# Attention scores on 64-row halves of TensorE's array, placed behind each step's transposes

## The chip, the cores and the metric

The kernel runs on one core of one Trainium2 chip. The time is device microseconds (us) of that core; lower is better. Before the change the median of three runs is 4348.14 us.

## What is computed

Two layers, each a group normalisation, an eight-head self-attention over 1024 positions and an output projection with a residual. The batch is 8, the channels 512, so a head has D = 64. All data are float32. One layer, cut to what matters (the second has another weight layout and the same mathematics):

```python
xn = group_norm(xf, norm_w, norm_b)                       # xf: (8, 512, 1024), 32 groups
qkv = einsum('oc,bct->bot', qkv_w, xn) + qkv_b            # 8 heads of q, k, v, 64 rows each
weight = softmax(einsum('bct,bcs->bts', q, k) / sqrt(64), axis=-1)
a = einsum('bts,bcs->bct', weight, v)
x = xf + einsum('oc,bct->bot', proj_w, a) + proj_b
```

## The kernel before

**Precision.** A float32 product is made from two fp32r parts, a high part (a rounded copy) and a low part (the rest), as three matmuls: high by high, high by low, low by high. So every tensor that TensorE multiplies has a `_hi` and a `_lo` form.

**Passes, pairs, steps, tiles.** A pass is one image in one layer: 2 x 8 = 16 passes (`Fori(0, PASSES)`). A pass has 8 heads in 4 pairs. Three pairs are run by an inner loop (`last` false), the fourth is written out (`last` true). So there are 48 loop pairs and 16 last pairs. A pair has 16 steps m (head e = 0 or 1, j = 0 to 7 in it), and a step is one tile of 128 queries against 1024 keys: 1024 tiles in all. Heads of Q and K for the head after next are projected in the loop pairs (`later_qk`, 3 matmuls a step, 6 in step 15); in the last pair a part of the output projection stands there in steps 0, 1, 14 and 15. A pass begins with the projections of V and of the first heads, and ends with the output projection.

**One tile's way.** TensorE writes the scores of tile m into half m % 2 of `ps_s`. DVE takes the row extreme (`smallest`, L560, `row_min`). ACT takes the exponential into `probs`, with the row sum by an accumulator read (`exponential`, L479). DVE takes the reciprocal (`reciprocal`, L564, `row_rcp`). POOL multiplies (`normalise`, L383). TensorE transposes the 1024 columns in 8 blocks into the two banks of `ps_t` (`transpose`, L760). ACT copies each bank as fp32r (`high_part`, L484, `pt_hi`, half 0 and half 1), DVE subtracts (`low_part`, L569, `pt_lo`, half 0 and half 1). After two tiles TensorE multiplies V with them into `ps_o` (`weigh`, L772 and L773, 8 matmuls a step from step 2 on; group 7 with 16 matmuls behind step 15). V stands with its high part in columns 0 to 63 and its low part in 64 to 127 (`v_st`), so `ps_o` holds two 64-row halves that must be added: ACT copies one (`other_half`, L491, `o_part`), DVE adds (`add_halves`, L578, `attn`), and then ACT and POOL split `attn` (`attn_high` L500, `attn_split` L407). For 4 of the 8 groups the sum goes to rows 0 to 63, for the others to rows 64 to 127.

**Scores before.** Q's high and low part are stacked to 128 rows (`q_st`), K's high part stands twice (`kh_st`) and K's low part stands twice (`kl_st`). Four matmuls of 128 x 512 make a tile's scores (L749 and L751, two column halves). POOL splits Q and K (`split_qk`, L370 and L372), and SP stacks them with two DMAs, a wait on them (`q_moved`), and two more (`stack`, L259 to L267); they write into the places that they read.

**Order.** It is written out by hand, the same in every engine. Each engine runs its own instructions strictly as listed and waits on semaphores. TensorE in step m: scores of tile m + 2, transposes of m, later Q and K, weigh. DVE in step m: (in even steps from 4 on, in a loop pair) `add_halves`; `smallest(m+2)`, `low_part(m, 0)`, `low_part(m, 1)`, `reciprocal(m+2)`. `scores` of m + 2 waits for the exponential of m; a transpose half waits for `low_part` of the tile before; `exponential(m+2)` waits for `smallest(m+2)`. ACT's order, which the change leaves as it is, is:

```python
                        if not last and m >= 4 and m % 2 == 0:
                            other_half(8 * pair + m // 2 - 2, m // 2 - 2)
                        high_part(tile + m, m, 0)
                        high_part(tile + m, m, 1)
                        if m == PT_STEPS - 1 or last and m >= 3 and m % 2 == 1:
                            other_half(8 * pair + (m - 3) // 2, (m - 3) // 2)
                        if not (last and m + 2 >= PT_STEPS):
                            exponential(tile + m + 2, m + 2, 2 * (tile + m) + 2)
                        if j in (3, 7) and not last:
                            evac_qk(hd + 2, col + hh + 2, j // 4, g_bank, True)
                        if j == 2 and not (last and e == 1):
                            v_high(hd + 1, hh + 1, 1 - e, 4 * hd)
                        if e == 1 and j in (4, 6):
                            attn_high(pair, p, (j - 4) // 2)
```

`evac_qk` (L466) takes the next Q and K out of PSUM, `v_high` (L473) copies V. Behind step 15 of a pair ACT has `attn_high(2)`, `other_half(7)` and `attn_high(3)`, DVE `add_halves(7)`. POOL in step m has at most one or two splits (`split_qk`, `split_wqk` L347 and L349, `v_low` L377, `attn_split`) and then `normalise(m+2)`. V's bias is added when V leaves PSUM (`evac_v`, L631, from `bv_all`).

Of the kernel before, what the change touches and what calls it, by code (L numbers as in the profile page):

```python
# [7 lines left out]
F32 = mybir.dt.float32  # L28
# [36 lines left out]
def build(nc, x, wqk, wv, wp, bqk, bv, bo, nw, nb, consts, out):  # L65
    mid = nc.dram_tensor("layer0_out", (B, C, T), F32, kind="Internal").ap()

    with ExitStack() as ctx:
# [34 lines left out]
        q_st = [sb(f"q_st{s}", [P, T], F32R) for s in range(2)]  # L103
        kh_st = [sb(f"kh_st{s}", [P, T], F32R) for s in range(2)]
        kl_st = [sb(f"kl_st{s}", [P, T], F32R) for s in range(2)]
# [8 lines left out]
        bv_all = sb("bv_all", [P, LAYERS, C], F32)  # L114
# [4 lines left out]
        bo_sb = sb("bo_sb", [P, LAYERS * KT], F32)  # L119
        nw_sb = sb("nw_sb", [P, LAYERS * KT], F32)  # L120
        nb_sb = sb("nb_sb", [P, LAYERS * KT], F32)
        qk_scale = sb("qk_scale", [P, 1], F32)
        row_min = sb("row_min", [P, 4], F32)
        row_sum = sb("row_sum", [P, 4], F32)
        row_rcp = sb("row_rcp", [P, 4], F32)
# [38 lines left out]
        q_moved = sem("q_moved")  # L164
# [81 lines left out]
        def _(sp):  # L246
# [34 lines left out]
            sp.dma_start(bv_all[:, :, :], bv.rearrange("(o l) n -> o l n", o=1).broadcast_to([P, LAYERS, C])).then_inc(const_loaded, 16)  # L281
# [61 lines left out]
        def _(pool):  # L343
# [22 lines left out]
            def split_qk(hd, s, half):  # L366
# [3 lines left out]
                nc.gpsimd.tensor_scalar(kh_st[s][:, cols], qk[:, cols], 1.0, 1.0, ALU.mult, ALU.mult).then_inc(qk_hi_done, 1)  # L370
                pool.wait_ge(qk_hi_done, 2 * hd + half + 1)
                nc.gpsimd.tensor_tensor(kl_st[s][:, cols], qk[:, cols], f32(kh_st[s][:, cols]),  # L372
# [183 lines left out]
        def _(dve):  # L556
# [15 lines left out]
            def add_halves(pair, k):  # L572
# [56 lines left out]
            def evac_v(i, lay, b):  # L629
# [34 lines left out]
            def pair_steps(i, p, last):  # L664
                pair = PAIRS * i + p
                tile = TILES * i + PT_STEPS * p
                for m in range(PT_STEPS):
                    if not last and m >= 4 and m % 2 == 0:
                        add_halves(pair, m // 2 - 2)
                    if not (last and m + 2 >= PT_STEPS):  # L670
                        smallest(tile + m + 2, m + 2)
                    low_part(tile + m, m, 0)
# [13 lines left out]
                add_halves(pair, 7)  # L686

            with dve.Fori(0, PASSES) as i:
                lay = i // B
                for b in range(4):  # L690
                    evac_v(i, lay, b)
                for m in range(2):
                    smallest(TILES * i + m, m)
                    evac_v(i, lay, 4 + 2 * m)
                    reciprocal(TILES * i + m, m)
                    evac_v(i, lay, 5 + 2 * m)
                with dve.Fori(0, PAIRS - 1) as p:
                    pair_steps(i, p, False)
# [237 lines left out]
```

## Time and profile before

| | |
|---|---|
| median of 3 runs | 4348.14 us (4347.87 to 4348.57) |
| span of the profiled execution, first to last instruction | 4346.0 us |
| matmuls (PE) | 26692, PE busy 99% |
| DVE, ACT, POOL busy | 76%, 66%, 58% |
| mean granted TensorE clock | 0.999 of full speed |

For the profiled execution the span is what is listed; the median of the runs lies 2.1 us above it. PE is TensorE's matmuls, PEld its weight loads, DVE VectorE, ACT ScalarE, POOL GpSimd, SP the engine that issues the DMAs. Busy shares are means over stages with different limits, so the rows below go to single stages. A matmul's duration overlaps the next one's, so the distance from start to start is what a matmul costs.

### The profile page before, as it was taken

Reading aid. Unit: us, or ns where it says so; the run is one execution under the profiler, and the core shown is the slowest. Engines: PE = TensorE matmul, PEld = TensorE weight load, DVE = VectorE, ACT = ScalarE, POOL = GpSimd, SP = SyncE. Lnnn points to the kernel's source line nnn. Section 1 sums busy time; section 2 is a strip of 40 time slices with the busy share of each in tenths; the row PEclk is TensorE's granted clock in tenths of the full one; section 3 lists DMA queues with packets and bytes.
Section 4 is the critical chain, followed back from the end, with each engine's and each line's share of the span. In section 5 each row is a group of like instructions: output and inputs, shape, how many; then the busy total and the mean of one; then the engine's idle time right before and its main releaser. Section 6 shows DMA issues by size and latency. Waiting matters only on the chain.

```text
span 4346.0 us, 89905 instructions
## 1 busy us (share of the span) xinstructions
PE 4295.6 (99%) x26692; PEld 3736.9 (86%) x26692; DVE 3313.6 (76%) x5483; ACT 2875.3 (66%) x5317; POOL 2505.1 (58%) x2406
## 2 busy tenths in 40 slices
PE   7999999999999999999999999999999999999999
PEld 6888888888888888888888888888888888888887
DVE  5777867788687786777867778687786877868778
ACT  4757747477474775747757476574765747667476
POOL 5655556565564655656566565565655646556465
PEclk9999999999999999999999999999999999999999
DMA  3232222322223222222222222222222222223222
GB/s 87 48 96 47 71 72 48 96 47 80 64 46 96 49 78 64 56 86 49 80 71 66 81 46 80 65 66 79 48 79 64 71 71 49 79 64 82 60 49 92
DMA packets 99933, 295.61 MB, mean 68 GB/s; under 512 B 15136, under 2 KB 15264, under 8 KB 99616
## 3 DMA queue, kind: packets, MB, share of 16 engines
q1 hardware_dynamic: 99616, 291.71, 25.0%
q8 instruction: 158, 2.59, 0.3%
q14 instruction: 159, 1.30, 0.1%
HBM read 123.88 MB, written 33.55 MB: 36 GB/s over the span
## 4 chain that ended last, share of the span: by engine, by line
PE 95%; DVE 2%; issue 1%; POOL 1%; ACT 1%; DMA 0%; SPq 0%; DVEq 0%; ACTq 0%; POOLq 0%
PE ps_t L760 21%; PE ps_g L714 15%; PE ps_o L772 11%; PE ps_o L773 11%; PE ps_s L751 11%; PE ps_s L749 11%; PE ps_s L714 7%; PE ps_t L714 6%; PE ps_o L714 3%; POOL x_raw L389 1%; ACT probs L479 0%; DVE spread L603 0%; DVE pt_lo L569 0%; DVE work L601 0%; PE ps_t L778 0%
## 5 line engine op out<-in xcount | busy, mean ns | idle before, releaser
L383 POOL TENSOR_SCALAR probs<-probs,row_rcp 128x1024 f32<-128x1024 f32 x1024 | 1149.9, 1123 | 1375.5 <-DVE row_rcp L564 1374.0
L560 DVE TENSOR_REDUCE row_min<-ps_s 128x1 f32<-128x1024 f32 x1024 | 1250.2, 1221 | 220.5 <-PE ps_s L751 205.0
L484 ACT CAST pt_hi<-ps_t 128x512 fp32r<-128x512 f32 x2048 | 1110.6, 590 | 446.5 <-PE ps_t L760 431.7
L569 DVE TENSOR_TENSOR pt_lo<-ps_t,pt_hi 128x512 fp32r<-128x512 f32 x2048 | 1308.5, 679 | 9.5 <-ACT pt_hi L484 5.0
L479 ACT ACTIVATE probs<-ps_s,row_min 128x1024 f32<-128x1024 f32 x1024 | 1150.7, 1124 | 215.5 <-DVE row_min L560 202.5
L760 PEld LDWEIGHTS ps_t<-const_sb,probs 128*128 128x128 f32 x8192 | 944.3, 140 | 185.5 <-DVE pt_lo L569 57.0
L760 PE MATMUL ps_t<-const_sb,probs 128*128 128x128 f32 x8192 | 1085.9, 274 | 0.8
L772 PE MATMUL ps_o<-pt_hi,v_st 128*128 128x256 f32 x4096 | 1044.4, 288 | 0.0
L773 PE MATMUL ps_o<-pt_lo,v_st 128*128 128x256 f32 x4096 | 1014.8, 282 | 0.0
L751 PE MATMUL ps_s<-kl_st,q_st 128*128 128x512 f32 x2048 | 808.3, 395 | 0.0
L772 PEld LDWEIGHTS ps_o<-pt_hi,v_st 128*128 128x128 f32 x4096 | 771.6, 188 | 39.4 <-issue 12.4
L749 PE MATMUL ps_s<-kh_st,q_st 128*128 128x512 f32 x2048 | 804.1, 393 | 0.0
L773 PEld LDWEIGHTS ps_o<-pt_lo,v_st 128*128 128x128 f32 x4096 | 774.4, 189 | 29.0
L751 PEld LDWEIGHTS ps_s<-kl_st,q_st 128*128 128x128 f32 x2048 | 388.0, 189 | 54.9
L578 DVE TENSOR_TENSOR attn<-ps_o,o_part 64x256 f32<-64x256 f32 x512 | 215.5, 421 | 281.3 <-ACT o_part L491 276.3
L749 PEld LDWEIGHTS ps_s<-kh_st,q_st 128*128 128x128 f32 x2048 | 386.0, 188 | 50.1 <-DMA kl_st<-kl_st 0.2
L714 PE MATMUL ps_g<-xn_hi,wqk_hi 128*128 128x512 f32 x768 | 352.8, 459 | 0.0
L372 POOL TENSOR_TENSOR kl_st<-qk,kh_st 128x512 fp32r<-128x512 f32 x256 | 329.6, 1287 | 21.4
L491 ACT COPY o_part<-ps_o 64x256 f32<-64x256 f32 x512 | 187.6, 366 | 186.2 <-PE ps_o L773 179.2
L564 DVE RECIPROCAL row_rcp<-row_sum 128x1 f32<-128x1 f32 x1024 | 167.5, 164 | 183.8 <-ACT probs L479 150.2
L714 PE MATMUL ps_g<-xn_hi,wqk_lo 128*128 128x512 f32 x768 | 307.2, 400 | 0.0
L714 PE MATMUL ps_g<-xn_lo,wqk_hi 128*128 128x512 f32 x768 | 304.3, 396 | 0.0
(110 smaller groups left out, 4918.2 us busy)
## 6 DMA issues: line engine op xcount, KB each, us to landing
wqk_raw<-in_wqk SPq DMA_DIRECT2D x130, 256.0 KB, 2.7
q_st<-kh_st SPq DMA_DIRECT2D x128, 256.0 KB, 2.9
q_st<-kl_st SPq DMA_DIRECT2D x128, 256.0 KB, 3.6
kh_st<-kh_st SPq DMA_DIRECT2D x128, 256.0 KB, 2.9
kl_st<-kl_st SPq DMA_DIRECT2D x128, 256.0 KB, 3.5
x_raw<-layer_out SPq DMA_DIRECT2D x36, 512.0 KB, 5.0
wv_raw<-in_wv SPq DMA_DIRECT2D x68, 256.0 KB, 3.6
x_raw<-in_x SPq DMA_DIRECT2D x32, 512.0 KB, 5.3
```

Source lines behind the costliest of these rows:

```text
L372: nc.gpsimd.tensor_tensor(kl_st[s][:, cols], qk[:, cols], f32(kh_st[s][:, cols]), ALU.subtract).then_inc(qk_split, 1)
L383: nc.gpsimd.tensor_scalar(probs[m % 2][:, :], probs[m % 2][:, :], row_rcp[:, m % 4:m % 4 + 1], 1.0, ALU.mult, ALU.mult).then_inc(probs_rea ...
L479: nc.scalar.activation(probs[m % 2][:, :], ps_s[:, m % 2, :], ACT.Exp, bias=row_min[:, m % 4:m % 4 + 1], scale=-1.0, accum_out=row_sum[:, ...
L484: nc.scalar.copy(pt_hi[:, m // 2 % 2, 4 * half:4 * half + 4, (m % 2) * P:(m % 2 + 1) * P], ps_t[:, half, :].rearrange("p (b t) -> p b t", ...
L560: nc.vector.tensor_reduce(row_min[:, m % 4:m % 4 + 1], ps_s[:, m % 2, :], AX.X, ALU.min).then_inc(min_ready, 1)
L569: nc.vector.tensor_tensor(pt_lo[place], ps_t[:, half, :].rearrange("p (b t) -> p b t", b=4), f32(pt_hi[place]), ALU.subtract).then_inc(lo_ ...
L714: return nc.tensor.matmul(bank, stat[hi_lo[0]](n // 3), mov[hi_lo[1]](n // 3), start=first, stop=last)
L749: nc.tensor.matmul(ps_s[:, m % 2, cols], q_st[s][:, j * P:(j + 1) * P], kh_st[s][:, cols], start=True, stop=False)
L751: mm = nc.tensor.matmul(ps_s[:, m % 2, cols], q_st[s][:, j * P:(j + 1) * P], kl_st[s][:, cols], start=False, stop=True)
L760: mm = nc.tensor.transpose(ps_t[:, half, b * P:(b + 1) * P], probs[m % 2][:, (4 * half + b) * P:(4 * half + b + 1) * P], ident)
L772: nc.tensor.matmul(ps_o[:, 0:GROUP], v, pt_hi[:, k % 2, b, :], start=(b == 0), stop=False)
L773: mm = nc.tensor.matmul(ps_o[:, 0:GROUP], v, pt_lo[:, k % 2, b, :], start=False, stop=(b == BLK - 1))
```

## The change

Scores: Q's and K's high parts stay as POOL writes them (`hi_st`: Q in rows 0 to 63, K in rows 64 to 127), the low parts too (`lo_st`), and four DMAs put swapped copies beside them (`hi_sw`, `lo_sw`), with no wait between. A tile's scores are six matmuls of 64 rows by 512 columns, in three pairs: one of a pair uses rows 0 to 63 of the array and makes columns 0 to 511, the other uses rows 64 to 127 and makes columns 512 to 1023. A pair is one of the three products.

Order: TensorE has `transpose(m)` ahead of `scores(m+2)`. DVE has `low_part(m, 0)`, `reciprocal(m+1)`, `smallest(m+2)`, `low_part(m, 1)`; the reciprocal of tile 1 of a pass moves from the head of the pass into step 0. ACT's and POOL's orders stay.

V's bias: no longer added to V, but to the sum of the halves (the probabilities of a row add up to 1), so `evac_v` becomes a copy and `add_halves` an operation with three inputs. The small tiles `qk_scale`, `row_min`, `row_sum`, `row_rcp` become slices of one, `row_stats`.

```diff
@@ SP, stack
-                sp.dma_start(f32(q_st[s][0:D, :]), f32(kh_st[s][0:D, :])).then_inc(q_moved, 16)
-                sp.dma_start(f32(q_st[s][D:P, :]), f32(kl_st[s][0:D, :])).then_inc(q_moved, 16)
-                sp.wait_ge(q_moved, 32 * (hd + 1))
-                sp.dma_start(f32(kh_st[s][0:D, :]), f32(kh_st[s][D:P, :])).then_inc(stacked[s], 16)
-                sp.dma_start(f32(kl_st[s][0:D, :]), f32(kl_st[s][D:P, :])).then_inc(stacked[s], 16)
+                for swapped, straight in ((hi_sw, hi_st), (lo_sw, lo_st)):
+                    sp.dma_start(f32(swapped[s][D:P, :]), f32(straight[s][0:D, :])).then_inc(stacked[s], 16)
+                    sp.dma_start(f32(swapped[s][0:D, 0:HALF]), f32(straight[s][D:P, 0:HALF])).then_inc(stacked[s], 16)
...
-            sp.dma_start(bv_all[:, :, :], bv.rearrange("(o l) n -> o l n", o=1).broadcast_to([P, LAYERS, C])).then_inc(const_loaded, 16)
+            sp.dma_start(bv_sb[:, :], bv).then_inc(const_loaded, 16)
@@ DVE, add_halves and evac_v
-                nc.vector.tensor_tensor(attn[rows, cols], ps_o[rows, 0:GROUP], o_part[k % 2][rows, :],
-                                        ALU.add).then_inc(attn_ready, 1)
+                nc.vector.scalar_tensor_tensor(out=attn[rows, cols], in0=ps_o[rows, 0:GROUP],
+                                               scalar=bv_sb[rows, bass.ds(lay * KT + p, 1)], in1=o_part[k % 2][rows, :],
+                                               op0=ALU.add, op1=ALU.add).then_inc(attn_ready, 1)
...
-                nc.vector.tensor_tensor(v_raw[:, b, :].rearrange("p (o n) -> p o n", o=1),
-                                        v_bank[b].rearrange("p (o n) -> p o n", o=1),
-                                        bv_all[:, bass.ds(lay, 1), :], ALU.add).then_inc(v_evac, 1)
+                nc.vector.tensor_copy(v_raw[:, b, :], v_bank[b]).then_inc(v_evac, 1)
@@ DVE, pair_steps
-                    if not (last and m + 2 >= PT_STEPS):
-                        smallest(tile + m + 2, m + 2)
                     low_part(tile + m, m, 0)
+                    if not (last and m + 1 >= PT_STEPS):
+                        reciprocal(tile + m + 1, m + 1)
+                    if not (last and m + 2 >= PT_STEPS):
+                        smallest(tile + m + 2, m + 2)
                     low_part(tile + m, m, 1)
                     if m == PT_STEPS - 1 or last and m >= 3 and m % 2 == 1:
-                        add_halves(pair, (m - 3) // 2)
-                    if not (last and m + 2 >= PT_STEPS):
-                        reciprocal(tile + m + 2, m + 2)
+                        add_halves(pair, lay, p, (m - 3) // 2)
@@ TensorE, scores
-                j = m % NT
-                for half in range(2):
-                    cols = slice(half * HALF, (half + 1) * HALF)
-                    nc.tensor.matmul(ps_s[:, m % 2, cols], q_st[s][:, j * P:(j + 1) * P], kh_st[s][:, cols],
-                                     start=True, stop=False)
-                    mm = nc.tensor.matmul(ps_s[:, m % 2, cols], q_st[s][:, j * P:(j + 1) * P], kl_st[s][:, cols],
-                                          start=False, stop=True)
+                tile = slice((m % NT) * P, (m % NT + 1) * P)
+                top, low = slice(0, D), slice(D, P)
+                first, second = slice(0, HALF), slice(HALF, T)
+                for n, (q, k) in enumerate(((0, 0), (1, 0), (0, 1))):
+                    nc.tensor.matmul(ps_s[:, m % 2, first], (hi_st, lo_st)[q][s][top, tile],
+                                     (hi_sw, lo_sw)[k][s][top, first], start=n == 0, stop=n == 2)
+                    mm = nc.tensor.matmul(ps_s[:, m % 2, second], (hi_sw, lo_sw)[q][s][low, tile],
+                                          (hi_st, lo_st)[k][s][low, second], start=n == 0, stop=n == 2)
                 mm.then_inc(scores_ready, 1)
@@ TensorE, pair_steps
+                        transpose(tile + m, m)
                         if not (last and m + 2 >= PT_STEPS):
                             pe.wait_ge(exp_ready, tile + m + 1)
...
                             scores(m + 2, s)
...
-                        transpose(tile + m, m)
```

How the change moves DVE's instructions shows in a step of a loop pair that has no `add_halves`. In these rows `ISA` and `REGISTER_ALU` are waits on semaphores and their counters, the rest are as named above. DVE before, from the `smallest` of one step to that of the next:

```order
L560 TENSOR_REDUCE row_min<-ps_s 128x1
L567 ISA
L569 TENSOR_TENSOR pt_lo<-ps_t,pt_hi 128x4x128
L567 REGISTER_ALU
L569 TENSOR_TENSOR pt_lo<-ps_t,pt_hi 128x4x128
L564 RECIPROCAL row_rcp<-row_sum 128x1
L559 REGISTER_ALU
L560 TENSOR_REDUCE row_min<-ps_s 128x1
```

DVE with the change, from the `low_part(m, 0)` of one step to the `smallest` of the next:

```order
L546 TENSOR_TENSOR pt_lo<-ps_t,pt_hi 128x4x128
L540 REGISTER_ALU
L541 RECIPROCAL row_stats<-row_stats 128x1
L536 REGISTER_ALU
L537 TENSOR_REDUCE row_stats<-ps_s 128x1
L544 REGISTER_ALU
L546 TENSOR_TENSOR pt_lo<-ps_t,pt_hi 128x4x128
L544 ISA
L546 TENSOR_TENSOR pt_lo<-ps_t,pt_hi 128x4x128
L541 RECIPROCAL row_stats<-row_stats 128x1
L536 REGISTER_ALU
L537 TENSOR_REDUCE row_stats<-ps_s 128x1
```

Before, the `smallest` stood ahead of both `low_part`s of its step; now one `low_part` and the reciprocal stand ahead of it and one `low_part` behind it.

TensorE before, from the end of one step's `weigh` to the `later_qk` of the next (`const_sb` is the identity that the transposes multiply with, and `x4` is four blocks):

```order
L773 MATMUL ps_o<-pt_lo,v_st_73 128x256
L811 REGISTER_ALU
L749 MATMUL ps_s<-kh_st_68,q_st_66 128x512
L751 MATMUL ps_s<-kl_st_70,q_st_66 128x512
L749 MATMUL ps_s<-kh_st_68,q_st_66 128x512
L751 MATMUL ps_s<-kl_st_70,q_st_66 128x512
L758 ISA
L760 MATMUL ps_t<-const_sb,probs_80 128x128 x4
L758 REGISTER_ALU
L760 MATMUL ps_t<-const_sb,probs_80 128x128 x4
```

TensorE with the change, the same stretch:

```order
L753 MATMUL ps_o<-pt_lo,v_st_75 128x256
L736 REGISTER_ALU
L738 ISA
L740 MATMUL ps_t<-const_sb,probs_83 128x128 x4
L738 REGISTER_ALU
L740 MATMUL ps_t<-const_sb,probs_83 128x128 x4
L729 MATMUL ps_s<-hi_sw_70,hi_st_66 128x512
L731 MATMUL ps_s<-hi_st_66,hi_sw_70 128x512
L729 MATMUL ps_s<-hi_sw_70,lo_st_68 128x512
L731 MATMUL ps_s<-hi_st_66,lo_sw_72 128x512
L729 MATMUL ps_s<-lo_sw_72,hi_st_66 128x512
L731 MATMUL ps_s<-lo_st_68,hi_sw_70 128x512
```

The scores moved behind the eight transposes, and four matmuls became six; L729 uses the array's upper rows and L731 its lower rows.

## Rows read from the trace of the kernel before

**Rows 1.** The page: span, PE busy, chain that ended last.

```profile
span 4346.0 us, 89905 instructions
...
PE 4295.6 (99%) x26692; PEld 3736.9 (86%) x26692; DVE 3313.6 (76%) x5483; ACT 2875.3 (66%) x5317; POOL 2505.1 (58%) x2406
...
PE 95%; DVE 2%; issue 1%; POOL 1%; ACT 1%; DMA 0%; SPq 0%; DVEq 0%; ACTq 0%; POOLq 0%
```

**Rows 2.** Windows table, loop pair and 14 last-pair steps: length, busy us (count), clock.

```profile
982.76:1038.05 55.29, 55.29 (x369) 49.32 (x368) 44.27 (x73) 43.57 (x82) 34.50 (x34) 1.00 0.22 53
1038.05:1078.68 40.63, 40.58 (x277) 34.81 (x275) 37.06 (x61) 34.33 (x65) 21.05 (x20) 1.00 0.35 110
```

**Rows 3.** Chain of waits, one step of a loop pair: start us, us, what.

```profile
1000.19 0.23 PE ps_s L749
...
1001.12 0.87 PE ps_t L760 x8
1002.00 0.69 PE ps_g L714 x3
1002.69 0.12 PE ps_o L772
...
1003.64 0.23 PE ps_s L749
```

**Rows 4.** Timeline of ACT, last pair: start us, us, operation [idle <-releaser].

```profile
1048.25 1.11 ACT L479 ACTIVATE probs<-ps_s,row_min 128x1024 f32<-128x1024 f32 x1
...
1049.36 1.06 ACT L484 CAST pt_hi<-ps_t 128x512 fp32r<-128x512 f32 x2
1050.84 1.12 ACT L479 ACTIVATE probs<-ps_s,row_min 128x1024 f32<-128x1024 f32 x1 [0.42 <-DVE row_min L560]
```

**Rows 5.** Timeline of DVE, a loop pair: low parts, reciprocal, smallest.

```profile
968.44 1.29 DVE L569 TENSOR_TENSOR pt_lo<-ps_t,pt_hi 128x512 fp32r<-128x512 f32 x2
969.68 0.16 DVE L564 RECIPROCAL row_rcp<-row_sum 128x1 f32<-128x1 f32 x1
969.78 1.23 DVE L560 TENSOR_REDUCE row_min<-ps_s 128x1 f32<-128x1024 f32 x1
```

**Rows 6.** Timeline of DVE, last pair: the smallest ahead of the exponential at 1050.84.

```profile
1049.59 1.22 DVE L560 TENSOR_REDUCE row_min<-ps_s 128x1 f32<-128x1024 f32 x1
```

**Rows 7.** Timeline of all engines, step 15: copy, waiting low part.

```profile
1081.13 1.07 ACT L484 CAST pt_hi<-ps_t 128x512 fp32r<-128x512 f32 x2 [1.08 <-PE ps_t L760]
...
1081.74 0.69 DVE L569 TENSOR_TENSOR pt_lo<-ps_t,pt_hi 128x512 fp32r<-128x512 f32 x1
```

**Rows 8.** Timeline of ACT: what else stands between exponential and copy.

```profile
981.31 0.36 ACT L491 COPY o_part<-ps_o 64x256 f32<-64x256 f32 x1 [0.84 <-PE ps_o L773]
...
982.76 1.07 ACT L484 CAST pt_hi<-ps_t 128x512 fp32r<-128x512 f32 x2
...
1007.10 0.79 ACT L466 ACTIVATE qk<-ps_g,bqk_sc,qk_scale 128x512 f32<-128x512 f32 x1
1007.92 0.37 ACT L491 COPY o_part<-ps_o 64x256 f32<-64x256 f32 x1
...
1045.91 0.61 ACT L473 CAST v_st<-v_raw 128x512 fp32r<-128x512 f32 x1
1046.47 1.07 ACT L484 CAST pt_hi<-ps_t 128x512 fp32r<-128x512 f32 x2
...
1075.43 0.39 ACT L500 CAST a_hi<-attn 128x256 fp32r<-128x256 f32 x1
1075.72 1.09 ACT L484 CAST pt_hi<-ps_t 128x512 fp32r<-128x512 f32 x2
```

**Rows 9.** The page: normalise on POOL, a score matmul, a stacking DMA.

```profile
L383 POOL TENSOR_SCALAR probs<-probs,row_rcp 128x1024 f32<-128x1024 f32 x1024 | 1149.9, 1123 | 1375.5 <-DVE row_rcp L564 1374.0
...
L751 PE MATMUL ps_s<-kl_st,q_st 128*128 128x512 f32 x2048 | 808.3, 395 | 0.0
...
kl_st<-kl_st SPq DMA_DIRECT2D x128, 256.0 KB, 3.5
```

More of the change, by code:

```diff
@@ L102, in build @@
         qk = sb("qk", [P, T], F32)
-        q_st = [sb(f"q_st{s}", [P, T], F32R) for s in range(2)]
-        kh_st = [sb(f"kh_st{s}", [P, T], F32R) for s in range(2)]
-        kl_st = [sb(f"kl_st{s}", [P, T], F32R) for s in range(2)]
+        hi_st = [sb(f"hi_st{s}", [P, T], F32R) for s in range(2)]
+        lo_st = [sb(f"lo_st{s}", [P, T], F32R) for s in range(2)]
+        hi_sw = [sb(f"hi_sw{s}", [P, T], F32R) for s in range(2)]
+        lo_sw = [sb(f"lo_sw{s}", [P, T], F32R) for s in range(2)]
         v_raw = sb("v_raw", [P, BLK, C], F32)
@@ L119, in build @@
         bo_sb = sb("bo_sb", [P, LAYERS * KT], F32)
+        bv_sb = sb("bv_sb", [P, LAYERS * KT], F32)
         nw_sb = sb("nw_sb", [P, LAYERS * KT], F32)
         nb_sb = sb("nb_sb", [P, LAYERS * KT], F32)
[L122 to L125, printed above, removed]
+        row_stats = sb("row_stats", [P, 16], F32)
+        qk_scale = row_stats[:, 12:13]
+        row_min, row_sum, row_rcp = (row_stats[:, 4 * n:4 * n + 4] for n in range(3))
         bn_part = sb("bn_part", [P, KT, 12], F32)
@@ L570, in low_part, with add_halves @@
                                         f32(pt_hi[place]), ALU.subtract).then_inc(lo_ready, 1)
-            def add_halves(pair, k):
+            def add_halves(pair, lay, p, k):
                 rows = slice(0, D) if k < 4 else slice(D, P)
@@ L662, in _, with pair_steps @@
                 x_low(0, c)
-            def pair_steps(i, p, last):
+            def pair_steps(i, lay, p, last):
                 pair = PAIRS * i + p
@@ L668, in pair_steps @@
                     if not last and m >= 4 and m % 2 == 0:
-                        add_halves(pair, m // 2 - 2)
+                        add_halves(pair, lay, p, m // 2 - 2)
+                    low_part(tile + m, m, 0)
+                    if not (last and m + 1 >= PT_STEPS):
+                        reciprocal(tile + m + 1, m + 1)
                     if not (last and m + 2 >= PT_STEPS):
                         smallest(tile + m + 2, m + 2)
-                    low_part(tile + m, m, 0)
                     low_part(tile + m, m, 1)
                     if m == PT_STEPS - 1 or last and m >= 3 and m % 2 == 1:
-                        add_halves(pair, (m - 3) // 2)
-                    if not (last and m + 2 >= PT_STEPS):
-                        reciprocal(tile + m + 2, m + 2)
+                        add_halves(pair, lay, p, (m - 3) // 2)
                     if last and m == PT_STEPS - 2:
@@ L685, in pair_steps @@
                     group_spread(i + 1)
-                add_halves(pair, 7)
+                add_halves(pair, lay, p, 7)
             with dve.Fori(0, PASSES) as i:
@@ L690, in _ @@
                 for b in range(4):
-                    evac_v(i, lay, b)
+                    evac_v(i, b)
                 for m in range(2):
                     smallest(TILES * i + m, m)
-                    evac_v(i, lay, 4 + 2 * m)
-                    reciprocal(TILES * i + m, m)
-                    evac_v(i, lay, 5 + 2 * m)
+                    evac_v(i, 4 + 2 * m)
+                    if m == 0:
+                        reciprocal(TILES * i, 0)
+                    evac_v(i, 5 + 2 * m)
                 with dve.Fori(0, PAIRS - 1) as p:
-                    pair_steps(i, p, False)
-                pair_steps(i, PAIRS - 1, True)
+                    pair_steps(i, lay, p, False)
+                pair_steps(i, lay, PAIRS - 1, True)
                 norm_coefs(i + 1, within(next_pass(i) // B, 0, LAYERS - 1))
@@ L858, in _ @@
                     qk_part(half, qk_bank[1][half], 1, 0, 3 * KT)
-                pe.wait_ge(stacked[0], 32 * (4 * i + 1))
+                pe.wait_ge(stacked[0], 64 * (4 * i + 1))
                 scores(0, 0)
```

12 lines of the change are left out of this document (5 added, 7 removed).

## The prediction, made before the changed kernel ran

> **What bounds the kernel now.** First the page: TensorE is busy 99% of the span and 95% of the chain that ended last [rows 1]. Such a share is a mean, so next the windows: TensorE is busy all of a loop pair's 55.29 us and nearly all of the 40.63 us of steps 0 to 13 of a last pair, at full clock (the column behind the busy times) [rows 2]. The chain of waits then gives one loop step by starts: scores 0.93 us (1000.19 to 1001.12), eight transposes 0.88, three matmuls for later Q and K 0.69, weigh 0.95, together 3.45 us [rows 3]. So in a loop pair each microsecond saved on TensorE is one saved, if nothing else is longer.
>
> In the last pair something else is nearly as long. There ACT sat idle for 0.42 us before the exponential at 1050.84, waiting for DVE's smallest [rows 4]. Here one must ask not how busy DVE and ACT are, but which of their instructions wait for each other in turn. Today the turn is: exponential, reciprocal, smallest of the next tile, exponential. It leaves out the copy and the low part, since DVE's list has the smallest ahead of them.
>
> **What the change does to TensorE.** A score matmul costs 0.23 us from start to start [rows 3]. Four become three pairs. If the halves run side by side, a tile's scores cost 3 x 0.23 = 0.69 instead of 0.93: 0.24 us less per tile, 1024 x 0.23 = about 236 us in all. If they run one after the other, six cost 1.38, 0.45 more. No row shows a 64-row matmul, so these two are my bounds; I take the first, but below it hardly counts. A change between full and half array may cost nothing or, by the nearest row, the tail by which a score matmul outlasts its start-to-start distance: 0.395 - 0.23 = 0.16 us [rows 3, 9], twice a step.
>
> **What it does to DVE and ACT.** This is the term that decides. DVE now has low_part(m, 0), reciprocal(m+1), smallest(m+2), low_part(m, 1). ACT still has copy(m, 0), copy(m, 1), exponential(m+2). Follow one turn: exponential(m+2) on ACT is ahead of copy(m+1, 0) on ACT; that is awaited by low_part(m+1, 0) on DVE; behind that in DVE's list are reciprocal(m+2) and smallest(m+3); and that is awaited by exponential(m+3). This is a ring of one step in which nothing can overlap, whatever TensorE does. Its length from rows:
> - exponential to next copy, start to start: 1.11 (1048.25 to 1049.36) [rows 4]
> - copy to a low part that waits for it: 0.61 (1081.13 to 1081.74) [rows 7]
> - low part to reciprocal: two low parts last 1.29 and one 0.69, so the second starts 0.60 behind the first, and the reciprocal 1.24 - 0.60 = 0.64 behind the second [rows 5, 7]
> - reciprocal to smallest: 0.10 [rows 5]
> - smallest to exponential: 1.25 (1049.59 to 1050.84) [rows 4, 6]
>
> Sum 3.71 us, against TensorE's new step of 0.69 + 0.88 + 0.69 + 0.95 = 3.21. The ring wins, and TensorE begins to wait.
>
> Whatever ACT does between an exponential and the next copy lengthens the ring. In a loop pair [rows 8]: four evacuations of Q and K at 0.8 (0.82 to the next start), 3.2; six other_half ahead of a copy at 0.4 (0.37 and its handover), 2.4; two copies of V at 0.56, 1.1; two of attn at 0.29, 0.6. add_halves on DVE runs beside the copy (0.61) and is hidden. At the pair's end: from copy(15, 0), the exponential of tile 17 starts at +2.60, the evacuation ends at +4.5, attn_high(2) at +4.8, and TensorE finishes group 7 at about +5.0 (an estimate: 0.88 + 0.69 + 0.95 + 6 x 0.23 + 16 x 0.12 = 5.8 of its work, begun some 0.8 ahead of the copy). Then other_half(7), add_halves(7), attn_high(3) to the next pair's copy take 1.45 as now (981.31 to 982.76). That is +6.45, where an ordinary step would be at +4.5: 1.95 more. One loop pair: 16 x 3.71 + 3.2 + 2.4 + 1.1 + 0.6 + 1.95 = 68.6 us, against 55.3: **+13.3, times 48 = +638**.
>
> Last pair, copy(0, 0) to copy(14, 0): 14 x 3.71 = 51.9, with one copy of V and one of attn 52.8, against 40.6 [rows 2]. The other_half there stands behind both copies, in ACT's time of waiting for the smallest, and is hidden. **+12.2, times 16 = +195**.
>
> **Edits that cost nothing.** evac_v and the first two tiles' scores lie at a pass's head, where DVE waits for TensorE: only the two score tiles count, -0.46 us a pass, -7. Should the copy be slower than the add, TensorE's next work there covers it. add_halves with a third input may be longer by a tenth (it has no row); the copy beside it has 0.2 to spare. The four stacking DMAs follow each other without the wait that stood between; one lands in 3.5 us [rows 9], and they have five steps. POOL's normalise waited 1374 us in all for the reciprocal [rows 9]: it will wait again, as its list is as before. The reciprocal now stands 0.10 ahead of the smallest, so normalise (1.12) is done while smallest and exponential run (2.36 to the copy), and the first transposes are just in time: some 0.4 us to spare. If that were used up, transposes would be late next. TensorE's spare time (about 0.5 a step) covers two array changes of 0.16.
>
> **Sum.** 4346 + 638 + 195 - 7 = 5172 us of span. The median of the runs stands 2 above the span of the profiled execution: 5174, and I say **5175**. Bounds of the ring: with every handover 0.02 shorter, 3.61; with the low part, the reciprocal and the smallest counted at full length 0.69 + 0.16 + 1.25 and 0.04 per handover, about 3.9. Over the 48 x 16 + 16 x 14 = 992 steps that is -100 and +190.
>
> **Rivals.**
> 1. *TensorE stays the bound, halves side by side.* The gain of 236 us then comes out: **4110 us, faster**. Place: each step's scores; price: 0.23; it decides once the ring is under 3.45. For it: the page, on which DVE and ACT have 24% and 34% free [rows 1]. Against it: free time in a ring can't be used. 4%.
> 2. *The ring holds and the halves do not run side by side* (the change doesn't do what it says). TensorE's step is 3.21 + 0.69 = 3.90, with two array changes of 0.16 4.22. In a loop pair about five of 16 steps carry nothing extra on ACT and are then set by TensorE: 240 steps x 0.2 to 0.5, +50 to +120 us, and more where the two chains couple: **about 5290**. For it: no row shows halves at all. 7%.
> 3. *TensorE stays the bound, and each array change costs its tail.* TensorE's step is 3.21 + 0.33, 0.09 longer than before: 4346 + 1024 x 0.09 = **about 4440, slower**. For it: the tail of 0.16 is in the rows. Against it: the ring is longer still. 3%.
>
> On this the Trainium skill has a rule, in "TensorEngine Tiling (Array Packing)", Key Properties under Tiling Modes: changing the tiling mode drains TensorE. By that rule rival 3 is how the change goes if only TensorE counts, and without the rule it is rival 1; the trace of before has only full-array matmuls and can't say. Beside the ring the rule changes nothing in the sum.
>
> **How the numbers follow.** The ring is a matter of the written order, and its parts are measured rows, so it gets 84% at 5175; 2% is left for what I don't see. The range takes in the ring's bounds and most of rival 2: 5060 to 5365. A measurement of this kernel can tell 0.2% (9 us) from no change. Faster 4% (rival 1), within 0.2% 1%, slower 95%.
>
> **What would show it.** Right: TensorE with idle time before the transposes or scores; ACT's copy waits little for TensorE; chains through exponential, copy, low part, smallest; the smallest-to-smallest distance in a last pair even, near 3.7 us; a loop pair near 68 us. Pairs of score matmuls starting close together and 0.23 us per pair show the halves side by side; 0.23 per matmul shows rival 2. Wrong: a loop pair under 56 us, or a chain that stays 90% TensorE, or copies that wait for transposes in most steps, which would put POOL's normalise in the ring's place.

## The result and the profile after

| | before | changed kernel |
|---|---|---|
| median | 4348.26 us (4347.87 to 4348.57, 4 runs) | 5235.68 us (5233.19 to 5238.03, 4 runs) |
| ratio | 1 | 1.2041, 95% interval 1.2024 to 1.2058 |
| span of the profiled execution | 4346.0 us | 5232.3 us |
| mean granted clock | 0.999 | 0.995 |

The change makes the kernel 887 us slower. The forecast was 5175, range 5060 to 5365.

The page of the changed kernel, against [rows 1, 9] (a group's columns: busy us, mean ns of one, idle us before them and their releaser):

```profile
span 5232.3 us, 94049 instructions
...
PE 4655.5 (89%) x28740; PEld 3547.1 (68%) x28740; DVE 3261.2 (62%) x5483; ACT 2854.5 (55%) x5317; POOL 2505.8 (48%) x2406
...
issue 28%; DVE 26%; PE 21%; ACT 17%; POOL 3%; ACTq 2%; DVEq 2%; DMA 0%; POOLq 0%; SPq 0%
...
L546 DVE TENSOR_TENSOR pt_lo<-ps_t,pt_hi 128x512 fp32r<-128x512 f32 x2048 | 1402.8, 686 | 927.6 <-ACT pt_hi L461 913.9
L456 ACT ACTIVATE probs<-ps_s,row_stats 128x1024 f32<-128x1024 f32 x1024 | 1143.4, 1117 | 1374.7 <-DVE row_stats L537 1366.7
L740 PE MATMUL ps_t<-const_sb,probs 128*128 128x128 f32 x8192 | 1114.0, 279 | 512.1 <-POOL probs L360 509.7
```

TensorE fell from 95% of the chain to 21%. DVE and ACT did not become busier: DVE is at 62% and ACT at 55%, less than before, yet together with "issue" (time in which an engine waited for nothing that the profile shows) they hold most of the chain. The three groups say who waits: the low part 914 us for the copy, the exponential 1367 us for the smallest, the transposes 510 us for the normalise. A ring in which each waits for the last looks like this. Before, the exponential waited 202.5 us in all for the smallest and the low part 5.0 for the copy.

Windows of the changed kernel, to be read against [rows 2]: two loop pairs, the stretch from a last pair's step 0 to the start of the next pass's second loop pair, and steps 0 to 13 of that last pair (length first, clock behind the counts):

```profile
1431.49:1500.42 68.93, 61.12 (x403) 46.09 (x400) 43.46 (x72) 43.45 (x82) 34.53 (x34) 1.00 0.12 31
1174.89:1245.01 70.12, 62.60 (x400) 47.22 (x400) 43.57 (x72) 43.58 (x83) 34.51 (x34) 0.98 0.13 38
1245.01:1431.49 186.48, 167.46 (x1000) 128.42 (x996) 114.80 (x196) 91.11 (x169) 85.48 (x80) 1.00 0.19 60
...
1245.01:1297.62 52.61, 43.23 (x298) 31.95 (x295) 37.24 (x62) 33.41 (x66) 22.79 (x22) 1.00 0.22 75
```

Between the starts of pairs, two loop pairs and the long stretch (last pair, output projection, head of the pass, first loop pair) make a pass. Over all that the trace shows, a loop pair went from 55.33 to 69.20 us (32 of each) and the long stretch from 158.67 to 186.40 (15 of each): 32 x 13.87 + 16 x 27.73 = 888, all of the loss. Of the 27.73, 13.87 is the loop pair in it and 11.98 are steps 0 to 13 of the last pair (40.63 to 52.61).

The ring, in a timeline of all engines of the changed kernel (start us, us, operation, [idle <-releaser]):

```profile
1132.66 1.12 ACT L456 ACTIVATE probs<-ps_s,row_stats 128x1024 f32<-128x1024 f32 x1 [1.46 <-DVE row_stats L537]
...
1132.96 1.09 PE L740 MATMUL ps_t<-const_sb,probs 128*128 128x128 f32 x8 [0.32 <-POOL probs L360]
...
1133.77 1.06 ACT L461 CAST pt_hi<-ps_t 128x512 fp32r<-128x512 f32 x2
...
1134.38 0.69 DVE L546 TENSOR_TENSOR pt_lo<-ps_t,pt_hi 128x512 fp32r<-128x512 f32 x1 [1.15 <-ACT pt_hi L461]
...
1134.98 0.15 DVE L541 RECIPROCAL row_stats<-row_stats 128x1 f32<-128x1 f32 x1
1135.06 1.20 DVE L537 TENSOR_REDUCE row_stats<-ps_s 128x1 f32<-128x1024 f32 x1
...
1136.29 1.11 ACT L456 ACTIVATE probs<-ps_s,row_stats 128x1024 f32<-128x1024 f32 x1 [1.46 <-DVE row_stats L537]
```

Read it as distances: exponential to copy 1.11, copy to low part 0.61, to reciprocal 0.60, to smallest 0.08, to the next exponential 1.23. That is 3.63 us for a step, and all of its links were named ahead. The copy at 1133.77 has no bracket: it waited for nothing but ACT's own exponential, although the transposes had begun only 0.81 ahead of it.

TensorE in the changed kernel, one step's transposes, scores and the first matmul for later Q and K:

```profile
1128.86 1.05 PE L740 MATMUL ps_t<-const_sb,probs 128*128 128x128 f32 x8
1129.84 0.49 PE L729 MATMUL ps_s<-hi_sw,hi_st 64*128 64x512 f32 x1
1129.84 0.49 PE L731 MATMUL ps_s<-hi_st,hi_sw 64*128 64x512 f32 x1
1130.17 0.39 PE L729 MATMUL ps_s<-hi_sw,lo_st 64*128 64x512 f32 x1
...
1130.73 0.50 PE L692 MATMUL ps_g<-xn_hi,wqk_hi 128*128 128x512 f32 x1
1131.07 0.40 PE L692 MATMUL ps_g<-xn_lo,wqk_hi 128*128 128x512 f32 x1
```

The halves do run side by side: both of a pair start within 0.01 us. But the first pair stands 0.33 ahead of the second (the next distance is 0.23), and the first full-array matmul behind them 0.34 ahead of the next, against 0.23 between such matmuls before. So TensorE's own step is 0.98 + 0.89 + 0.80 + 0.95 = 3.62 us here (transposes, scores, later Q and K, weigh), not 3.21, and not less than the 3.45 of before. Two things are thus to be separated: the ring and the halves.

### The profile page after: what moved, and what is told of

Same layout as the page of the kernel before. It is cut to its first block, busy times and chain, and to the rows that moved or that the text cites. A ratio compares the mean times of both kernels' runs of the same rounds, so it can differ in the third digit from the quotient of the medians.

```text
span 5232.3 us, 94049 instructions
## 1 busy us (share of the span) xinstructions
PE 4655.5 (89%) x28740; PEld 3547.1 (68%) x28740; DVE 3261.2 (62%) x5483; ACT 2854.5 (55%) x5317; POOL 2505.8 (48%) x2406
## 4 chain that ended last, share of the span: by engine, by line
issue 28%; DVE 26%; PE 21%; ACT 17%; POOL 3%; ACTq 2%; DVEq 2%; DMA 0%; POOLq 0%; SPq 0%
DVE row_stats L537 19%; ACT pt_hi L461 9%; PE ps_s L692 5%; ACT probs L456 5%; PE ps_t L692 4%; PE ps_o L752 2%; DVE row_stats L541 2%; PE ps_t L740 2%; ACT o_part L468 2%; PE ps_o L692 2%; PE ps_s L729 2%; POOL probs L360 2%; PE ps_g L692 2%; PE ps_o L753 2%; DVE pt_lo L546 1%
## 5 line engine op out<-in xcount | busy, mean ns | idle before, releaser
L360 POOL TENSOR_SCALAR probs<-probs,row_stats 128x1024 f32<-128x1024 f32 x1024 | 1151.3, 1124 | 2335.4 <-DVE row_stats L541 2335.4
L456 ACT ACTIVATE probs<-ps_s,row_stats 128x1024 f32<-128x1024 f32 x1024 | 1143.4, 1117 | 1374.7 <-DVE row_stats L537 1366.7
L537 DVE TENSOR_REDUCE row_stats<-ps_s 128x1 f32<-128x1024 f32 x1024 | 1234.9, 1206 | 101.5 <-PE ps_s L731 101.0
L729 PE MATMUL ps_s<-hi_sw,hi_st 64*128 64x512 f32 x1024 | 510.5, 499 | 0.0
L731 PE MATMUL ps_s<-hi_st,hi_sw 64*128 64x512 f32 x1024 | 509.8, 498 | 0.0
L729 PE MATMUL ps_s<-hi_sw,lo_st 64*128 64x512 f32 x1024 | 404.7, 395 | 0.0
L731 PE MATMUL ps_s<-hi_st,lo_sw 64*128 64x512 f32 x1024 | 404.3, 395 | 0.0
L729 PE MATMUL ps_s<-lo_sw,hi_st 64*128 64x512 f32 x1024 | 402.9, 393 | 0.0
L731 PE MATMUL ps_s<-lo_st,hi_sw 64*128 64x512 f32 x1024 | 402.6, 393 | 0.0
L349 POOL TENSOR_TENSOR lo_st<-qk,hi_st 128x512 fp32r<-128x512 f32 x256 | 328.9, 1285 | 21.4
```

The lines of the kernel that those rows point to most:

```text
L349: nc.gpsimd.tensor_tensor(lo_st[s][:, cols], qk[:, cols], f32(hi_st[s][:, cols]), ALU.subtract).then_inc(qk_split, 1)
L360: nc.gpsimd.tensor_scalar(probs[m % 2][:, :], probs[m % 2][:, :], row_rcp[:, m % 4:m % 4 + 1], 1.0, ALU.mult, ALU.mult).then_inc(probs_rea ...
L456: nc.scalar.activation(probs[m % 2][:, :], ps_s[:, m % 2, :], ACT.Exp, bias=row_min[:, m % 4:m % 4 + 1], scale=-1.0, accum_out=row_sum[:, ...
L537: nc.vector.tensor_reduce(row_min[:, m % 4:m % 4 + 1], ps_s[:, m % 2, :], AX.X, ALU.min).then_inc(min_ready, 1)
L729: nc.tensor.matmul(ps_s[:, m % 2, first], (hi_st, lo_st)[q][s][top, tile], (hi_sw, lo_sw)[k][s][top, first], start=n == 0, stop=n == 2)
L731: mm = nc.tensor.matmul(ps_s[:, m % 2, second], (hi_sw, lo_sw)[q][s][low, tile], (hi_st, lo_st)[k][s][low, second], start=n == 0, stop=n == 2)
```

## Experiments

Each is named by what it is made from. Single times are one execution, those with a range are several.

**1. Before, with DVE's new order alone.**

```diff
+                    low_part(tile + m, m, 0)
+                    if not (last and m + 1 >= PT_STEPS):
+                        reciprocal(tile + m + 1, m + 1)
                     if not (last and m + 2 >= PT_STEPS):
                         smallest(tile + m + 2, m + 2)
-                    low_part(tile + m, m, 0)
                     low_part(tile + m, m, 1)
                     if m == PT_STEPS - 1 or last and m >= 3 and m % 2 == 1:
                         add_halves(pair, (m - 3) // 2)
-                    if not (last and m + 2 >= PT_STEPS):
-                        reciprocal(tile + m + 2, m + 2)
...
-                    reciprocal(TILES * i + m, m)
+                    if m == 0:
+                        reciprocal(TILES * i, 0)
```

> The kernel before, with DVE's new order alone (low part 0, reciprocal of the next tile, smallest, low part 1); scores on the full array, TensorE's order as before. Theory of the ring (exponential, copy, low part, reciprocal, smallest, exponential, 3.63 us in the trace of the change): it is closed by DVE's order alone, so about 5200 us (5130 to 5260), smallest to smallest 3.63 us in plain steps. Rival, that the halves and the array changes around them cost the time: no halves here, so within 1% of 4348 us.

Measured: 5180.7 us. On its page TensorE is busy 89%, DVE 62% and ACT 55%, as in the change. Its waits (us in total, times, longest):

```profile
ACT probs L479 <- DVE row_min L560: 1484.8, 1024, 5.1
DVE pt_lo L569 <- ACT pt_hi L484: 925.8, 832, 1.7
```

Moving one low part and the reciprocal in DVE's list costs 832 of the 887 us, with TensorE's work untouched. A loop pair lasts 68.61 us, and a step in which ACT has nothing extra 3.63 to 3.64 from copy to copy.

**2. Before, with both new orders, full array** (experiment 1, and `transpose(m)` ahead of `scores(m+2)`).

> The change without the halves and without the moved bias: full-array scores, but the transposes ahead of the scores and DVE's new order. Ring: 5190 to 5240 us, as the change, since TensorE's step of 3.45 us is under the ring. Rival (halves are what costs): within 1% of 4348 us; a rival that the placement behind the transposes costs by itself shows as more than e1_new_dve_order_alone by over 50 us.

Measured: 5194.3 us. Putting the transposes first costs another 13 us. These are two single executions, but their traces agree: a loop pair is as long (68.66 us), and the long stretch goes from 184.16 to 184.88, 12 us over 16 passes. From here to the change, halves and bias add 41.

**3. The change, with both orders as before** (halves and moved bias stay).

> The change with TensorE's and DVE's orders as before: what halves and moved bias do by themselves. Ring: it is open again, TensorE binds, and a step costs what its work costs. In the trace of the change a step of TensorE's work is 3.62 us against 3.45 before, so about 4500 us (4440 to 4560), loop pairs near 58 us. If array changes cost less where the scores stand between weigh and transposes, down to 4110. Rival (halves are what costs): over 5000 us.

Measured: 4450.8 us (4449.5 to 4454.4, 4 runs), ratio 1.0233 (1.0216 to 1.0250). The chain of waits in a loop step, against [rows 3]:

```profile
2007.65 0.43 PE ps_s L728
...
2008.08 0.23 PE ps_s L728
...
2008.55 1.02 PE ps_t L739 x8
2009.57 0.70 PE ps_g L691 x3
...
2011.22 0.43 PE ps_s L728
```

TensorE holds 94% of this chain, so here its step decides: 3.57 us against 3.45. Three pairs would be 0.69; they take 0.89, since the first costs 0.43. The transposes behind them take 1.02 where they took 0.87. The two changes between full and half array cost 0.20 + 0.15 = 0.35, the halves give back 0.24.

**4. The bias alone** (before, with V's bias added in `add_halves`; the rest of the edit, the copy in `evac_v` among it, is cut here).

```diff
-                nc.vector.tensor_tensor(attn[rows, cols], ps_o[rows, 0:GROUP], o_part[k % 2][rows, :],
-                                        ALU.add).then_inc(attn_ready, 1)
+                nc.vector.scalar_tensor_tensor(out=attn[rows, cols], in0=ps_o[rows, 0:GROUP],
+                                               scalar=bv_sb[rows, bass.ds(lay * KT + p, 1)], in1=o_part[k % 2][rows, :],
+                                               op0=ALU.add, op1=ALU.add).then_inc(attn_ready, 1)
```

> The kernel before, with V's bias moved alone (copy out of PSUM, three-input add of the halves). Theory: hidden, 4348 us within 0.2%; the add of the halves takes 0.06 us longer as in the trace of the change (0.48 against 0.42), which no ring of before contains except at a pair's end (64 pairs x 0.06 = 4 us at most). Rival (the bias explains part of the 100 us that halves and bias together cost): 4370 us or more.

Measured: 4360.6 us (10 runs), ratio 1.0022 (1.0012 to 1.0031). That is 9 us over the 4351.5 of before in the same batch, and 12 over the 4348.8 of experiment 3's batch. It was to be hidden, 4 us at most, so this missed by a little. The add with three inputs takes 0.48 us against 0.42 in the groups by line, and a loop pair 55.56 against 55.33. So some 10 of experiment 3's 102 us are the bias, some 90 the halves.

**5. Experiment 3, with all six score matmuls on rows 0 to 63** (the DMAs then move the whole of K's swapped copy; that edit is not shown).

```diff
-                    mm = nc.tensor.matmul(ps_s[:, m % 2, second], (hi_sw, lo_sw)[q][s][low, tile],
-                                          (hi_st, lo_st)[k][s][low, second], start=n == 0, stop=n == 2)
+                    mm = nc.tensor.matmul(ps_s[:, m % 2, second], (hi_st, lo_st)[q][s][top, tile],
+                                          (hi_sw, lo_sw)[k][s][top, second], start=n == 0, stop=n == 2)
```

> Halves with both old orders, but all six matmuls of a tile on rows 0 to 63 (K's swapped copy is moved whole, so nothing is left out). If the two halves of the array really work side by side, taking that away costs 3 x 0.23 us a tile: 4451 + 1024 x 0.69 = 5157 us (5080 to 5180). Rival (the pairs' equal starts in the trace are only how matmuls are recorded, and they run one after the other): 4451 us unchanged.

Measured: 5147.6 us. TensorE's timeline in this kernel:

```profile
1100.98 0.50 PE L728 MATMUL ps_s<-hi_sw,hi_st 64*128 64x512 f32 x1
1101.32 0.39 PE L730 MATMUL ps_s<-hi_sw,hi_st 64*128 64x512 f32 x1
```

On the same rows the six follow one by one, the first 0.34 ahead of the second, the others 0.22 to 0.24 apart. That makes the kernel 697 us longer than experiment 3, near the 1024 x 0.69 = 707 of three matmuls more a tile. So it is the two row halves that let a pair share its 0.23.

**6 and 7. Four array changes a step instead of two, and the control.** Experiment 3 and the kernel before, each with its scores cut in two around the matmuls for later Q and K (one pair and two pairs; two matmuls and two). In experiment 3 (cut; the old place of `later_qk` is taken out and `scores` gets a range):

```diff
-                            scores(m + 2, s)
+                            scores(m + 2, s, 0, 1)
+                            if not last and m < PT_STEPS - 1:
+                                later_qk(i, m, hd, e, j)
+                            scores(m + 2, s, 1, 3)
```

> Halves with both old orders, and in loop pairs the three matmuls for later Q and K stand between the first pair of score matmuls and the other two: four array changes a step instead of two, the same matmuls. If two changes cost what the books say (0.24 gained, 0.12 lost in all, so 0.36 for two), 48 x 15 steps x 0.36 = 260 us more than e3_halves_both_orders_old, 4710 us (4640 to 4760), less what the same reordering costs with full-array scores (e8_full_split_around_qk). Rival (the loss comes from elsewhere, such as weight loads or DVE): no more than that control's difference.

> Control for e7_halves_split_around_qk: the kernel before, full-array scores, with the three matmuls for later Q and K between the two column halves of the scores. No array change at all, so what it costs is the reordering: 0 to 2 us a loop pair (the wait for the evacuation of Q and K comes 1.3 us earlier in four steps), 4348 to 4440 us.

Measured: 4917.8 us with halves, 4558.2 us for the control. The control missed: it was to cost at most 92 us and cost 210. Its waits (us in total, times, longest) say why:

```profile
PEld ps_g L714 <- ACT qk L466: 217.7, 144, 1.5
```

The matmuls for later Q and K now come before ACT has emptied their bank. With halves the same wait is 207.0 us, so it can be taken off. What is left for the array changes is the difference: halves cost 4917.8 - 4558.2 = 360 us with four changes a step and 4450.8 - 4348.8 = 102 with two. Those 258 us over the 720 steps of loop pairs in which the scores are cut (48 x 15) are 0.36 us for two more changes. In steps where nothing waits for the bank the traces give it without the control's loss: with halves a step goes from 3.57 to 3.97 us, in the control from 3.45 to 3.44, so 0.40 or 0.41 for two more changes. The change's own step (0.10 in the transposes, 0.20 in the scores, 0.11 in later Q and K over what they would take) gives 0.41. With the 0.35 of experiment 3's chain, two changes cost 0.35 to 0.41 us.

**8. The change, with DVE's order as before** (TensorE's transposes stay first).

> The change with DVE's order as before and TensorE's as changed (transposes ahead of scores). The ring between ACT and DVE is open, but the low part of a tile now stands behind the smallest of a tile whose scores come after the transposes: transposes 0.98, scores 0.89, arrival 0.2, smallest to low part 1.14, low part 0.69, together 3.9 us before the next transposes may start. So 4750 to 4950 us, loop pairs near 63 us, with transposes waiting for low parts. Rival (order does not matter): 5235 us as the change.

Measured: 5259.0 us. A clear miss: undoing what costs 832 us by itself gained nothing here. The timeline of all engines in this kernel:

```profile
1130.40 1.25 PE L739 MATMUL ps_t<-const_sb,probs 128*128 128x128 f32 x8 [0.30 <-DVE pt_lo L546]
...
1131.58 0.49 PE L728 MATMUL ps_s<-hi_sw,hi_st 64*128 64x512 f32 x1
...
1132.58 1.23 DVE L537 TENSOR_REDUCE row_stats<-ps_s 128x1 f32<-128x1024 f32 x1 [1.40 <-PE ps_s L730]
...
1133.73 1.28 DVE L546 TENSOR_TENSOR pt_lo<-ps_t,pt_hi 128x512 fp32r<-128x512 f32 x2
...
1134.46 1.25 PE L739 MATMUL ps_t<-const_sb,probs 128*128 128x128 f32 x8
```

This is another ring: transposes, scores (+1.18), smallest (+1.00), low part (+1.15), next transposes (+0.73), 4.06 us. The expectation had named it, with 3.9 us; the last pairs keep to it (56.08 us for 14 steps), but a loop pair takes 68.8 where 63 was expected, and why its steps with extra work on ACT and DVE take 4.4 to 5.05 was not traced. DVE has the smallest ahead of the low parts, TensorE the transposes ahead of the scores, so the transposes wait for a low part, that for the smallest, that for the scores, and those for the transposes. That a low part waits for the smallest holds only while DVE's smallest stands ahead of both low parts; with the new DVE order one low part stands ahead of it. So DVE's new order closes one ring, TensorE's new order with DVE's old one another, and the parts' costs don't add up. TensorE's new order alone on the full array was not run.

**9. The change, with a shorter smallest** (512 columns; it leaves out half of each row's search, so the exponential's shift comes from half a row).

```diff
-ps_s[:, m % 2, :], AX.X, ALU.min)
+ps_s[:, m % 2, 0:HALF], AX.X, ALU.min)
```

> The change, with the smallest taken over the first 512 of the 1024 columns (this leaves half of each row's search out; the exponential's shift then comes from half a row). One member of the ring is shortened by about 0.53 us (1.22 to 0.69, the length of DVE's other operations on 512 columns), nothing on TensorE. Theory of the ring: a plain step falls from 3.63 to 3.10 in the last pairs, where TensorE's work is below that; in loop pairs TensorE's own step of about 3.6 us takes over in plain steps and the ring stays where ACT has extra work, so 60 to 62 us a loop pair. In all about 4700 us (4640 to 4800). Rival (DVE is only 62% busy and so cannot bind): 5235 us within 1%.

Measured: 4965.9 us. Taking 0.53 us out of one link of the ring gained 270 us: the link is in the bound. But more was expected, and the timeline of this kernel shows what stopped it:

```profile
1201.74 0.15 DVE L541 RECIPROCAL row_stats<-row_stats 128x1 f32<-128x1 f32 x1
...
1202.10 1.12 POOL L360 TENSOR_SCALAR probs<-probs,row_stats 128x1024 f32<-128x1024 f32 x1 [2.83 <-DVE row_stats L541]
...
1203.35 1.09 PE L740 MATMUL ps_t<-const_sb,probs 128*128 128x128 f32 x8 [0.83 <-POOL probs L360]
...
1204.04 1.07 ACT L461 CAST pt_hi<-ps_t 128x512 fp32r<-128x512 f32 x2 [0.32 <-PE ps_t L740]
...
1205.27 0.15 DVE L541 RECIPROCAL row_stats<-row_stats 128x1 f32<-128x1 f32 x1
```

Right behind the first ring lies a second, reciprocal, normalise, transposes, copy, low part, reciprocal: 3.53 us, against 3.63 for the first. It holds no exponential, so ACT's extra work is not in it, and this is where most of the gain lies: from copy to copy a plain loop step went only from 3.64 to 3.53, one with `other_half` from 4.15 to 3.69. Loop pairs give 5.4 x 48 = 260 of the 270 us; the 14 steps of a last pair hardly moved (52.60 to 52.04).

**10. Before, with the same shorter smallest.**

> The kernel before, with the same smallest over 512 columns (half of each row's search left out). Loop pairs are bound by TensorE and stay at 55.3 us; in the last pairs the short ring (exponential, reciprocal, smallest) loses up to 0.5 us a step and TensorE's 2.67 us takes over from 2.92: 14 x 16 x 0.22 = 50 us less, 4300 us (4280 to 4335). Rival (no ring bound the last pairs either): 4348 us within 0.2%.

Measured: 4310.8 us, beside 4347.2 for before. Where TensorE binds, the same saving is worth 36 us, in the last pairs and the passes' heads; a loop pair stays at 55.1.

**11 and 12. The late reciprocal alone**: before (11), and experiment 3 (12), with `reciprocal(m+1)` directly behind `smallest(m+2)`, the low parts behind both.

> The kernel before, with one move in DVE's order: the reciprocal of tile m+1 stands behind smallest(m+2) instead of the reciprocal of m+2 at the end of step m. The shorter ring of the last pair (exponential, reciprocal, smallest, exponential, 2.59 us, seen as 2.92 us a step) is opened, and TensorE's step there is 2.67 us. Theory of rings: the 14 steps of each last pair lose up to 0.25 us, so 4290 to 4330 us. Rival (TensorE alone sets the time of before): 4348 us within 0.2%.

> The change with TensorE's order as before and DVE with smallest(m+2), reciprocal(m+1), low part 0, low part 1. e3_halves_both_orders_old plus the move of e5: if the short ring binds the last pairs, 20 to 60 us under 4451 us; if with halves TensorE binds there too, 4451 us within 0.3%.

Measured: 4449.0 us, ratio 1.0228 (1.0211 to 1.0245), and 4525.5 us, ratio 1.0408 (1.0390 to 1.0425). Both missed: a gain, or at worst nothing, was expected, and it cost 100 us, 75 on top of the halves. In experiment 11 some 88 of the 100 are in loop pairs (55.33 to 57.16 us, times 48), and nearly all of that in the four distances from copy 0, 4, 8 and 12 to the next, the steps behind an evacuation of Q and K on ACT. The timeline of all engines in one of them:

```profile
961.90 0.14 DVE L564 RECIPROCAL row_rcp<-row_sum 128x1 f32<-128x1 f32 x1
...
962.25 1.12 POOL L383 TENSOR_SCALAR probs<-probs,row_rcp 128x1024 f32<-128x1024 f32 x1 [1.78 <-DVE row_rcp L564]
...
963.51 1.09 PE L761 MATMUL ps_t<-const_sb,probs 128*128 128x128 f32 x8
```

POOL stood idle for 1.78 us, waiting for the reciprocal. TensorE's transposes start 0.14 behind the end of this normalise and 0.21 later than the scores ahead of them allow (the last of those starts at 963.07). In a last pair it can be a split on POOL behind the late reciprocal that does the same: there one normalise starts at 1069.64, at the end of a split, and the transposes at 1070.89. The waits also give 223 us of transposes held by low parts. This is read from the trace; no run tests it by itself, nor how the 100 us divide between the two.

## Why the prediction was right, and where its terms were off

**The ring decides: shown.** Experiment 1 changes nothing but DVE's list and gives 5180.7. The likeliest case named this ring and no other; rival 1 (4110) needed a step under 3.45, rival 2 needed halves one after the other, which experiment 5 excludes. Rival 3 (4440) is what happens without the new order: experiment 3 gave 4450.8.

**The ring's length.** 3.71 forecast, 3.63 measured; no link is off by more than 0.04.

**Loop pair.** 68.6 forecast, 68.61 in experiment 1, 69.20 in the change. The close hit is partly two errors against each other: 16 x 0.08 = 1.3 less for the ring, and a pair's end longer than forecast. ACT there, in the changed kernel:

```profile
1167.41 1.07 ACT L461 CAST pt_hi<-ps_t 128x512 fp32r<-128x512 f32 x2
...
1173.38 0.36 ACT L468 COPY o_part<-ps_o 64x256 f32<-64x256 f32 x1 [1.26 <-PE ps_o L753]
1174.39 0.41 ACT L477 CAST a_hi<-attn 128x256 f32 x1 [0.65 <-DVE attn L556]
1174.89 1.07 ACT L461 CAST pt_hi<-ps_t 128x512 fp32r<-128x512 f32 x2
```

Copy to copy it takes 7.48, where I had 6.45. TensorE finishes group 7 at about +6, not +5.0: its estimate had everything back to back, but here it also stood still for 0.33 and paid for the array change. The halves are the small part of it: in experiment 1, without them, the mean of the same distance is 7.32, against 7.42 in the change.

**Last pair.** 52.8 forecast, 52.61 measured, again with two errors: the ring was taken 0.08 a step too long, and "the other_half there [...] is hidden" failed. ACT in a last pair, against [rows 4]:

```profile
1278.69 1.06 ACT L461 CAST pt_hi<-ps_t 128x512 fp32r<-128x512 f32 x2
1281.05 0.37 ACT L468 COPY o_part<-ps_o 64x256 f32<-64x256 f32 x1 [1.29 <-PE ps_o L753]
1281.44 1.12 ACT L456 ACTIVATE probs<-ps_s,row_stats 128x1024 f32<-128x1024 f32 x1
...
1282.55 1.06 ACT L461 CAST pt_hi<-ps_t 128x512 fp32r<-128x512 f32 x2
...
1286.18 1.06 ACT L461 CAST pt_hi<-ps_t 128x512 fp32r<-128x512 f32 x2
```

A step without it is 3.63 (1282.55 to 1286.18), one with it 3.86, because `other_half` itself waits for TensorE. This comes with the halves: in experiment 1 such steps take 3.63 like the others and the 14 steps 51.69, as forecast but for the ring's 0.08 a step, and in experiment 2 they take 3.69. Step 15 was no term at all: from copy(14, 0) to copy(15, 0) it takes 3.52, against 2.45 before, as normalise and its transposes come late there too: 16 x 1.07 = 17 us.

**Halves: the term that failed.** They were to bring 7 us, with TensorE's spare time covering the array changes. Halves and bias cost 41 us on top of the ring, and 102 where TensorE binds. The side-by-side gain of 0.24 was right; the changes cost 0.20 and 0.15, against at most 0.16 each, and the step grew to 3.62, as long as the ring, so nothing was left to cover them. The Trainium skill says in "TensorEngine Tiling (Array Packing)", Key Properties under Tiling Modes, that changing the tiling mode drains TensorE. Experiment 3's chain, with 0.35 us for a step's two changes, and experiments 6 and 7, with 0.36 to 0.41, show a cost at each change, as a drain would make; the traces do not show the drain itself.

**Bias and normalise.** The bias was taken as free and costs some 10 us. The transposes were to have 0.4 to spare; the second ring of 3.53 leaves 0.10.

**The sum.** Measured less forecast is 61 us: 12 from loop pairs at full clock (68.86 against 68.6, times 48), 16 from the clock (below), 17 from step 15, -3 from the last pairs, and some 20 for the rest of a pass, which is forecast at -7. That is 62, within the rounding of these readings.

## What to carry to other kernels

Walk the rings before you trust a busy share: write each engine's in-order list side by side and follow "waits for" and "stands behind" until you come back to the same instruction one step later; the sum of start-to-start distances along it is a floor for the step, here 3.63 us with DVE at 62% and ACT at 55%. A reordering that only lets something start earlier on one engine can close such a ring with a list on another, and an order that is right beside one list is wrong beside another: DVE's old order gives 4450.8 us with TensorE's old order and 5259.0 with its new one (experiments 3 and 8). A link's worth ends where the next ring begins (experiment 9). Row halves give 0.24 us per tile here and two array changes take 0.35 to 0.41, so two tiles' scores between changes would be needed for a gain; that is an estimate from these numbers and was not tried. None of these kernels that computes everything beat the kernel before.

## What was not expected of the hardware

A change between full-array and 64-row matmuls is not free in either direction: 0.20 us into the halves and 0.15 out of them (experiment 3's chain). Whether it is the array that must empty or the next weights that load late is not separated by any run.

A short idle stretch was followed by a lower clock in some loop pairs and not in others. At the start of a loop pair TensorE stands idle for 1.72 us, waiting for the normalise. The eight transposes behind that wait, in two loop pairs of the changed kernel (TensorE's timeline):

```profile
1177.73 1.81 PE L740 MATMUL ps_t<-const_sb,probs 128*128 128x128 f32 x8 [1.72 <-POOL probs L360]
...
1434.33 1.09 PE L740 MATMUL ps_t<-const_sb,probs 128*128 128x128 f32 x8 [1.72 <-POOL probs L360]
```

In the first the granted clock is at 0.50 of full speed, 1.2 GHz. Windows of 1 us there, with the clock third from the end:

```profile
1178.00:1179.00 1.00, 1.00 (x7) 1.00 (x6) 0.00 (x0) 0.91 (x3) 0.98 (x2) 0.50 0.00 0
...
1182.00:1183.00 1.00, 0.57 (x5) 0.33 (x3) 0.98 (x2) 0.58 (x1) 0.92 (x2) 1.00 0.00 0
```

It stays there for some 3.4 us. Of the 32 loop pairs seen, 13 last 69.29 to 70.40 us and the other 19 from 68.75 to 68.96; the mean of all is 0.34 above that of the 19, about 16 us over 48. The windows of the 13 read a clock of 0.98, those of the 19 read 1.00. The same idle stretch at 1432 to 1434 left the clock alone; what tells the two apart stays open.
